# A POOL memset of 112 columns behind each of the 270 indirect transfers of a macaron block

## The reference, cut to what matters

```python
x = x + 0.5 * _L0_ffn_ref(_layernorm(x), ...)   # int8-quantised linear layer, "q" in the kernel
x = x + _L0_attn_ref(_layernorm(x), ...)        # rms norm, conv, gated scan, gated ffn, "f"
x = x + 0.5 * _L0_ffn_ref(_layernorm(x), ...)   # "q", second time
x = x + 0.5 * _L1_ffn_ref(_layernorm(x), ...)   # mixture of experts, pass 1
x = x + _L1_attn_ref(_layernorm(x), ...)        # gated linear attention, "g"
x = x + 0.5 * _L1_ffn_ref(_layernorm(x), ...)   # mixture of experts, pass 2
```

```python
shared = _expert(x, Wg_s, Wu_s, Wd_s)
probs = jax.nn.sigmoid(jnp.einsum('bsh,eh->bse', x, Wr) + rb)
scores, idx = jax.lax.top_k(probs, 2)
cw = (jax.nn.one_hot(idx, 8) * scores[..., None]).sum(-2)
out = shared
for e in range(8):
    out = out + cw[..., e:e + 1] * _expert(x, Wg[e], Wu[e], Wd[e])   # 128 -> 256 -> 128, silu gate
```

## Time and profile before

| | |
|---|---|
| median of 3 runs | 683.96 us (683.24 to 685.11) |
| span of the profiled execution, first to last instruction | 692.3 us |
| what the profile gives around the span | nothing beside it |
| PE busy | 600.1 us, 87% of the span |
| DVE busy | 497.2 us, 72% |
| POOL busy | 419.3 us, 61% |
| ACT busy | 387.7 us, 56% |
| mean granted TensorE clock | 0.972 of full speed |
| scatters (L840) | 128, busy 128.1 us, POOL idle before them 72.2 us |
| stores (L1132) | 98 + 44, busy 96.3 + 43.7 us, POOL idle before them 57.5 + 49.0 us |

### The profile page before, as it was taken

How to read it: one execution, slowest core, us unless ns; L and a number is a source line. 1 busy time by engine, 2 the same in 40 slices (tenths; PEclk the granted TensorE clock), 3 DMA queues, 4 the chain that set the end, 5 groups by cost and what they waited for, 6 DMA issues and landing times.

```text
span 692.3 us, 14370 instructions
## 1 busy us (share of the span) xinstructions
PE 600.1 (87%) x4124; PEld 476.3 (69%) x4124; DVE 497.2 (72%) x1721; ACT 387.7 (56%) x1019; POOL 419.3 (61%) x445
## 2 busy tenths in 40 slices
PE   0366999999989998999897899999999999978974
PEld 0224565655666797888696686769879989857863
DVE  7997999978998865557224798989877766553335
ACT  2395968988766545444353728466565355533541
POOL 5276696488567777567643614553776575775552
PEclk9996999999999999999999999999999999999997
DMA  7999000001033355666768600124216556566796
GB/s 258 410 411 371 0 1 1 1 0 32 13 99 94 97 156 161 186 193 180 211 176 245 235 6 1 35 66 131 74 43 172 153 151 177 161 182 189 231 297 232
DMA packets 60125, 100.97 MB, mean 146 GB/s; under 512 B 10288, under 2 KB 28592, under 8 KB 59792
## 3 DMA queue, kind: packets, MB, share of 16 engines
q1 hardware_dynamic: 50832, 81.52, 38.5%
q0 software_dynamic: 8640, 17.84, 7.4%
q10 hardware_dynamic: 576, 0.69, 0.3%
HBM read 61.79 MB, written 38.23 MB: 144 GB/s over the span
## 4 chain that ended last, share of the span: by engine, by line
PE 43%; DVE 13%; DMA 9%; issue 6%; POOL 3%; SPq 2%; ACT 2%; POOLq 0%; DVEq 0%; ACTq 0%
PE bank L1083 13%; PE bank L1058 6%; PE bank L1296 5%; DMA tin<-rows_by_expert 3%; PE bank L969 3%; PE bank L955 3%; PE bank L944 2%; DMA hid<-rows_done 2%; DMA rows_done<-tout,tdst 2%; PE bank L1064 2%; DMA rows_done<-tout,tin 1%; POOL rows_by_expert L840 1%; DVE qt L417 1%; PE bank L312 1%; PE bank L307 1%
## 5 line engine op out<-in xcount | busy, mean ns | idle before, releaser
L840 POOL DMA_INDIRECT rows_by_expert<-xx,sidx x128 | 128.1, 1001 | 72.2 <-issue 34.0
L1083 PE MATMUL bank<-tint,twt 128*128 128x128 f32 x1136 | 151.8, 282 | 6.0 <-DVE thidt L1121 3.4
L1083 PEld LDWEIGHTS bank<-tint,twt 128*128 128x128 f32 x1136 | 141.1, 196 | 22.0 <-issue 12.3
L1132 POOL DMA_INDIRECT rows_done<-tout,tin x98 | 96.3, 983 | 57.5 <-ACT tout L1107 34.8
L1121 DVE TENSOR_TENSOR thidt<-tsil,bank 128x256 f32<-128x256 f32 x142 | 58.2, 418 | 95.8 <-ACT tsil L1099 74.1
L1099 ACT ACTIVATE tsil<-bank 128x256 f32<-128x256 f32 x142 | 53.9, 384 | 89.9 <-PE bank L1083 88.4
L1058 PE MATMUL bank<-e_dn,thidt 128*128 x568 | 90.6, 286 | 15.5 <-DVE thidt L1121 7.3
L1058 PEld LDWEIGHTS bank<-e_dn,thidt 128*128 128x128 f32 x568 | 76.8, 195 | 25.2 <-issue 24.8
L1107 ACT ACTIVATE tout<-bank,tin 128x128 f32<-128x128 f32 x142 | 50.2, 366 | 62.9 <-PE bank L1064 43.7
L1132 POOL DMA_INDIRECT rows_done<-tout,tdst x44 | 43.7, 993 | 49.0 <-ACT tout L1107 35.9
L1296 PEld LDWEIGHTS bank<-bufA,bufB 128*127 128x127 f32 (+6 forms) x448 | 47.7, 176 | 11.6 <-issue 6.7
(11 more groups left out here) (272 smaller groups left out, 1331.0 us busy)
## 6 DMA issues: line engine op xcount, KB each, us to landing
twt<-moe_gu SPq DMA_DIRECT2D x142, 256.0 KB
rows_by_expert<-tout SPq DMA_DIRECT2D x25, 715.0 KB, 20.0
tin<-rows_by_expert SPq DMA_DIRECT2D x142, 65.0 KB, 2.6
hid<-rows_done SPq DMA_DIRECT2D x12, 512.0 KB, 5.5
x<-x_in SPq DMA_DIRECT2D x8, 256.0 KB, 4.4
rows_by_expert<-xx,sidx POOLq DMA_INDIRECT x128
out<-x SPq DMA_DIRECT2D x8, 256.0 KB, 3.9
rows_done<-tout,tin POOLq DMA_INDIRECT x98
```

The lines of the kernel that those rows point to most:

```text
L840: pool.indirect_dma_start(out=rows_by_expert, out_offset=bass.IndirectOffsetOnAxis(ap=sidx[h][:, k:k + 1], axis=0), in_=xx[h][:, r, t, :], ...
L1083: m = pe.matmul(bank[UP_BANKS[p][j]][:, c * P:(c + 1) * P], weights[:, c * P:(c + 1) * P], tint[g % TURNS][:, :], start=True, stop=True)
L1132: pool.indirect_dma_start(out=rows_done, out_offset=bass.IndirectOffsetOnAxis(ap=dst, axis=0), in_=tout[:, g % RING, :], in_offset=None).t ...
```

## The change

A scratch tile `pause` of 128 partitions by 112 float32 columns is allocated. Behind every scatter and every store POOL clears it, and through `pool_step` waits until this memset is done before its stream goes on. Nothing reads the tile. No other instruction is added, removed or moved.

```diff
+PAUSE = 112
...
         tdst = sb("tdst", [P, RING], I32)
+        pause = sb("pause", [P, PAUSE])
         tout = sb("tout", [P, RING, P])
...
                 pool.indirect_dma_start(out=rows_by_expert, out_offset=bass.IndirectOffsetOnAxis(
                     ap=sidx[h][:, k:k + 1], axis=0), in_=xx[h][:, r, t, :], in_offset=None).then_inc(s_scat[h], 16)
+                pool_step(pool, pool.memset(pause[:, :], 0.0))
...
             pool.indirect_dma_start(out=rows_done, out_offset=bass.IndirectOffsetOnAxis(ap=dst, axis=0),
                                     in_=tout[:, g % RING, :], in_offset=None).then_inc(s_st[g % RING], 16)
+            pool_step(pool, pool.memset(pause[:, :], 0.0))
```

## The result

The changed kernel takes 763.17 us (median of 4 runs, 761.69 to 764.87) against 683.6 us for the kernel before in the same comparison (4 runs): ratio 1.116, 95% interval 1.1137 to 1.1183, or 79.6 us more. The forecast was 768 us.

The account below looks back on a forecast made before the run. It took PE as busiest (87% of the span, 43% of the chain), with POOL, 61% busy, nearly full in the stretches that start each pass's last wave. Pass 1's 43 us plus pass 2's 41 gave 84 on 684: 768 us, range 722 to 812.

Parts of the forecast that it names:

- the cover: On POOL, a transfer's 0.8 us preparation lies beside the transfer before, only 0.30 us showing; the new wait ends that.
- The memset: Behind each POOL transfer: 112 columns take 0.19 us, starting 0.03 us after the transfer.
- Price of a store: Each back-to-back store on POOL: 2.09 us instead of 1.26, so 0.82 us more.
- Price of an ordinary scatter: The other seven scatters of a unit on POOL: 0.46 us more each, bounds 0.18 and 0.83.
- the scatters are prepared ahead: Rival on ordinary scatters: only a semaphore instruction holds preparation back; 0.18 us each, 747 us in all; chance 0.15.
- the scatters pay like stores: Rival on ordinary scatters: a wait on the transfer stops preparation too; 0.83 us each, 796 us in all; chance 0.25.
- Pass 1, 333.3 to 500 us: POOL between the counted stretches of both passes: nothing carried over from before 500 us, so 0 us added.
- Waits of the second order: SP, ACT and PE waiting for POOL's late stores and scatters: not in the sum, pointing upward.
- The base: Profile span 692.3 us against runs' median 683.96: the 8.3 us difference carried unchanged, span about 776, time 768 us.
- The shared port: Memsets slowed by POOL's SBUF interfaces shared with VectorE: 0.1 us each, some 20 us more, left out of the sum.
- Not slower: Rival on POOL: memset and wait stay under the 0.30 us gap behind a transfer; 680 us; chance 0.04.
- Only the memset: Rival on POOL: preparation runs ahead behind every memset wait; about 0.24 us a transfer, 701 us; chance 0.12.

Follow-up runs that it names:

- e4b: Changed kernel with memsets taking turns over four fields, each waiting only for the memset four back, no transfer waiting for a memset: 696.05 us, ratio 1.0142.
- e3: Changed kernel with each wait for a memset moved onto the next transfer itself, behind any semaphore instruction: 706.64 us, ratio 1.0326.
- second profile of the kernel before: The kernel before run once more, unchanged, for its profile: 684.72 us, ratio 0.9991, profiled span 683.9 us.
- e8b: Kernel before, no memsets, with stores' waits for ACT and first scatters' waits for DVE moved from the semaphore instruction onto the transfer: 684.23 us, ratio 0.9966.

## Why the prediction was right, and by what luck

The main step of the forecast is shown: the fresh wait on POOL's own memset, where a semaphore instruction carries it, opens a gap of 0.82 us ahead of the transfer where 0.30 stood, and that, not the 0.21 us of memset, is most of the cost. That the gap is the transfer's preparation is argued only. For the 112 ordinary scatters the forecast said the cover is gone as well, and there it is not. Taken apart by the runs, of 79.6 us about 10 are the memsets without a fresh wait (e4b, 5 to 15), some 12 the wait where it sits on the transfer (e3 less e4b, no surer than that), and 56.5 the wait where it sits on the semaphore instruction ahead (changed less e3).

Step by step, the shift of the same POOL instruction between the second profile of the kernel before and that of the changed one:

| Stretch (times of before) | forecast, us | measured, us | with the measured prices, us |
|---|---|---|---|
| carried in at 244.4 | 6 | 3.5 | 2.8 |
| 244.4 to 333.3 | 36.9 | 29.2 | 26.0 |
| 333.3 to 500 | 0 | 14.8 | not counted |
| 500 to 586.1 | 15.9 | 12.6 | 7.7 |
| 586.1 to 622 | 17.0 | 11.6 | 12.0 |
| 622 to 683 | 9 | 5.7 | 6.0 |
| sum | 84 | 77.4 | 54.5 |

The forecast's column adds up to 84.8 and was rounded down at each step (9.3 - 1.7 - 1.0 is 6.6, not 6, and 2.09 - 1.26 is 0.83, not 0.82). The last column repeats the forecast's own counts with 0.73, 0.77 and 0.19 us: 33 x 0.73 + 4 x 0.77 + 28 x 0.19 - 6.5 = 26.0, for example. The measured column hangs on single instructions; between neighbours that waited and did not, the shift differs by up to 5 us.

- **The memset**: forecast 0.19 us and a start 0.03 us behind the transfer; measured 0.21 and 0.00 to 0.01. Right.
- **Price of a store**: forecast 0.82, measured 0.73. The gap of 0.82 us behind the wait is exact. What was off is the transfer behind it: I took 1.05 us from the earlier trace rows, where it stands behind an elementwise step. Behind a memset it takes 0.96 to 0.97.
- **Price of an ordinary scatter**: forecast 0.46, measured 0.19. This term failed. The gap of 0.45 us in the earlier trace rows was read as what a transfer needs behind a wait for `s_pl`; it was another case: there the wait stood on L351, and the scatter followed 0.17 us behind that. Of the rivals, "the scatters are prepared ahead" was right about this term (0.18, made of 0.17 + 1.05 where 0.28 + 0.96 was measured), and "the scatters pay like stores" is excluded by every row of 0.28. Its total of 747 us was nonetheless further off than 768.
- **Pass 1, 333.3 to 500 us**: forecast nothing, measured 14.8 us. This is the other step that failed, with the opposite sign. I counted the tail of pass 2 (33 stores, 9 us) but not that of pass 1, where the second profile of before has 30 stores behind the last scatter, to 397 us. By then the shift is 44.3 instead of 32.7 us, so 11.6 of the 14.8 us fall there. Yet counting it the same way would not have found them: 30 x 0.73 = 21.9 us against 27.4 + 5.9 - 30 x 0.30 = 24.3 us of idle time leaves nothing. What failed is the rule that POOL's idle time takes a delay up. The 18 stores of the last wave among the 30, in the second profile of before:

```profile
L1132 POOL DMA_INDIRECT rows_done<-tout,tdst x18 | 18.3, 1017 | 27.4 <-ACT tout L1107 21.9 <-issue 3.2 <-DVE tdst L1113 2.3
```

  Most of that wait for ACT is still there in the changed kernel, 16.9 of the 21.9 us. The first 20 of the 30 stores took the shift to 45.4 us. Ahead of the last ten POOL stood idle 23.2 us before and still 20.1 after: the steps of ACT that they wait for had moved along, so that idle time was no slack. In the tail of pass 2 the count came out (5.7 against 6.0); why one tail gives its idle time and the other not, no run separates.
- **Waits of the second order**: named, unpriced and pointed upward. They are there: SP waits 79.9 us for landings of stores instead of 18.4, PE 29.6 us for `tin` instead of 3.3. PE's clock was left out too: its mean granted clock went from 0.975 to 0.949, and the same 4124 matmuls are busy 620.0 us instead of 597.4. Beside pass 1's end the table leaves 77.4 - 54.5 - 14.8 = some 8 us. Some 3 of these are the next point's; another 4.9 (12.6 less 7.7) lie between 500 and 586.1 us. How much of them is waits and how much clock, the runs do not split.
- **The base**: I carried 8.3 us between the profile's span and the runs' median as if it lay in the method. It was one long execution, and a span is 1.8 us under its time. It did not touch the difference of 84 us, but the idle times in the rows were those of the long execution: from 244.4 to 333.3 us has 15.3 us ahead of the stores, the same stretch of the second profile 12.4, with 10.7 ahead of the scatters in both. The slack there is 23.1 - 19.5 = 3.6 us and not 6.5, and the measured prices then give 28.9 us against the 29.2 measured. So this stretch is accounted for.
- **The shared port**: the rule of the Trainium skill, GPSIMD Engine Reference, section Specifications, on SBUF interfaces shared with VectorE was left out of the sum. The median of the memsets is 206 ns, 205 at the least, so here it cost next to nothing. Only two of the 270 took longer than 0.23 us, 1287 ns (158.85 us, behind a scatter) and 416 ns (239.00, behind a store), and both ran while DVE worked on L434, a step with one SBUF input. The 31 that ran beside L1317, L1319, L1165, L1166 or L607, steps of DVE with two SBUF inputs, stayed at 0.21 us. The 755 ns of L349 in the earlier trace rows, which reads SBUF, did stand beside such a step: L605 of DVE started with it, at 120.98 us.
- **"Not slower"** (680 us) needed memset and wait inside the gap of 0.30 us. Behind a memset without a fresh wait they come to 0.38 us (e4b), behind one with it to 0.49 at the least. Excluded.
- **"Only the memset"** (701 us, 0.24 us a transfer): the trace excludes it for the stores of this kernel. For the ordinary scatters, at 0.19, it held, and e3, where every transfer carries its wait itself, came to 706.64 us. Where the wait is old, as in e4b, it is cheaper still. The Trainium skill, DMA: Bandwidth & Descriptors, section Anatomy of one DMA — SWDGE (gpsimd) path, has dispatch near 50 ns; the smallest gap ahead of a transfer in the rows shown is 0.17 us, and the transfer itself keeps POOL for 0.96 us.

As forecast, stores are some 2 us apart (2.1 said), POOL's busy time rose by 56 us (70 said), and the last scatter of pass 1 starts at 362.24 us (forecast 376). So 768 us came out close because prices too high by some 30 us met about 23 us that were not counted. The answer was right, and so was the mechanism for the stores, which carry most of it; for the scatters it was wrong, and the closeness was luck.

## What to carry to other kernels

Put a wait that is met late on the indirect transfer itself, not on an instruction ahead of it: here 0.28 against 0.82 us, 56 us over the kernel where it stood in full stretches, and nothing that could be told where POOL had slack (e8b). An engine at 61% busy may have next to no slack in the stretches that decide, so count its spacing there, gap included. And idle time behind another engine's step is slack only if that step does not move along with the delay: ask what that engine itself waits for.

## What was not expected of the hardware

- A memset behind an indirect transfer, without a fresh wait, costs much less than it takes: 0.21 us of memset widened the spacing by 0.07 us (e4b), as the gap behind a transfer shrinks from 0.30 to 0.17 us.
- An indirect transfer right behind a fresh wait on a semaphore instruction starts 0.79 to 0.85 us after the wait is met, for POOL's own semaphore, ACT's and DVE's alike; with the wait on the transfer, 0.27 to 0.28.
- Two profiled executions of one kernel differed by 8 us of span (692.3 and 683.9), through waits between 283 and 366 us.
- The same kernel took 684 and 800 us in different sets of runs, the longer time with stops of ACT, DVE and SP of up to 13 us that no record explains.
